# A one-core transformer layer on Trainium2: a rewritten drain, single signals, and two transposes in front of the first feed-forward product

## The reference

```python
# x: ids (128, 128); D = 64, four heads of 16, hidden 256
h = tok(x)        # 3 table rows per id -> 3 products + gelu -> fused product + gelu
                  # -> layer norm -> * (id != 0);  h = item_emb + 0.1 * fused
h = h + attn(layernorm(h))     # per sequence: softmax(q k^T / 4) v, then Wo
x3 = layernorm(h)
weights = x3 @ wr + br                        # one number per token
_, idx = top_k(weights, 64); sel = idx[:63]   # the 63 largest of a sequence's 128
y = gelu(x3[sel] @ w1 + b1) @ w2 + b2
out = h + x3;  out[sel] += y * weights[sel]
```

## Time and profile before

| | us |
|---|---|
| median of 3 runs | 552.93 |
| lowest, highest | 550.33, 558.99 |
| the profiled execution's own time | 557.61 |
| its span, first to last instruction | 555.7 |
| PE busy | 456.0 (82%) |
| DVE busy | 420.0 (76%) |
| ACT busy | 377.8 (68%) |
| POOL busy | 350.6 (63%) |

### The profile page before, as it was taken

The page is one execution under the profiler, slowest core; times in us unless marked ns, Lnnn a source line. Parts: engine busy times, 40 slices in busy tenths (PEclk is TensorE's granted clock), DMA queues, the critical chain, the costliest instruction groups (busy, mean ns, idle before and its releaser), DMA issues. The chain is left out here.

```text
span 555.7 us, 16674 instructions
## 1 busy us (share of the span) xinstructions
PE 456.0 (82%) x5850; PEld 346.8 (62%) x5850; DVE 420.0 (76%) x1648; ACT 377.8 (68%) x662; POOL 350.6 (63%) x412
## 2 busy tenths in 40 slices
PE   4778788888898888988988988888988789968670
PEld 2445576676666566766666666666767666756460
DVE  1367788877877888888777777888886658887486
ACT  1236677787877777777877778777776667846550
POOL 5746676676666676666766676667666547541574
PEclk9788999999999999999999999999997889998855
DMA  3211111111111111111111111111111111000046
GB/s 96 31 21 28 27 21 19 26 23 23 23 23 23 23 17 18 18 17 23 23 23 23 23 23 23 23 17 18 18 17 21 23 20 14 13 2 3 21 122 162
DMA packets 23733, 15.72 MB, mean 28 GB/s; under 512 B 18848, under 2 KB 21536, under 8 KB 23712
## 3 DMA queue, kind: packets, MB, share of 16 engines
q0 software_dynamic: 6144, 9.97, 12.1%
q1 hardware_dynamic: 17568, 5.48, 3.7%
HBM read 10.98 MB, written 4.19 MB: 27 GB/s over the span
## 5 line engine op out<-in xcount | busy, mean ns | idle before, releaser
L335 POOL TENSOR_TENSOR rs<-ve,minus_half 128x4 f32<-128x4 f32 x96 | 103.8, 1091 | 68.6 <-DVE ve L677 67.2
L327 POOL DMA_INDIRECT G<-table,idx x64 | 66.2, 1034 | 57.6 <-issue 47.7
L770 DVE TENSOR_REDUCE neg_max<-psum 128x4 f32<-128x512 f32 x128 | 84.4, 680 | 5.4 <-PE psum L1124 5.4
L327 POOL DMA_INDIRECT G<-turned,idx x64 | 60.7, 948 | 19.5 <-issue 19.5
L1052 PE MATMUL psum<-wt,hid 128*128 128x64 f32 x512 | 69.8, 294 | 2.5 <-ACT hid L471 1.5
L464 ACT ACTIVATE prob<-psum 128x512 f32<-128x512 f32 x128 | 66.1, 602 | 5.3 <-PE psum L1094 3.5
L1052 PEld LDWEIGHTS psum<-wt,hid 128*128 128x128 f32 x512 | 66.1, 208 | 3.3 <-ACT hid L471 2.2
L1094 PE MATMUL psum<-q_s,k_s 32*128 32x128 f32 x1024 | 39.1, 288 | 28.6 <-issue 23.5
L1094 PEld LDWEIGHTS psum<-q_s,k_s 32*128 32x128 f32 x1024 | 33.4, 191 | 35.5 <-issue 29.2
L814 DVE TENSOR_SCALAR k_s<-psum,wt 128x512 f32<-128x512 f32 x32 | 24.0, 751 | 31.7 <-PE psum L1211 31.0
L1124 PE MATMUL psum<-k_s,q_s 32*128 32x128 f32 x1024 | 41.1, 301 | 3.5 <-ACT prob L464 3.5
(11 more groups left out here) (116 smaller groups left out, 1108.5 us busy)
## 6 DMA issues: line engine op xcount, KB each, us to landing
out<-R SPq DMA_DIRECT2D x13, 256.0 KB, 2.6
G<-table,idx POOLq DMA_INDIRECT x64
G<-turned,idx POOLq DMA_INDIRECT x64
wt<-packed SPq DMA_DIRECT2D x1, 932.0 KB, 4.8
q_s<-max_t SPq DMA_DIRECT2D x32, 8.0 KB
out<-R SPq DMA_DIRECT2D x1, 512.0 KB, 4.3
out<-R SPq DMA_DIRECT2D x2, 128.0 KB, 3.5
ids_sb<-ids SPq DMA_DIRECT2D x1, 64.0 KB, 1.9
```

The costliest lines, as they stand in the source:

```text
L327: pool.indirect_dma_start(G[par][:, b, :], None, turned if b >= 2 else table, bass.IndirectOffsetOnAxis(ap=idx[par][:, b:b + 1], axis=0),) ...
L335: pool.tensor_tensor(rs[:, :], ve[:, :], minus_half[:, :], ALU.pow).then_inc(S[dst], 1)
L770: dve.tensor_reduce(neg_max[:, GB * h:GB * h + GB], bank[h].rearrange("p (b k) -> p b k", b=GB), AX, ALU.max, negate=True).then_inc(S["max ...
```

## The change

1. *Order on PE.* In a step `attention_t` and `fused_t` stand in front of `ffn_first`, which stood ahead of them.
2. *Single signals.* `scores`, `scores_back`, `queries`, `keys` and `ffn_first` signal once, at their last matmul, where they signalled four, four, two, two and four times; the waits count accordingly.
3. *Where the loops end.* PE's and DVE's loops end at step 17 (SPLIT = 18) and steps 18 to 29 are written out on both. ACT, POOL and SP keep theirs.
4. *Routing in three parts.* Part 0 is now columns 0 to 63 and is ranked by DVE inside the written-out steps: weights taken in step 18, one round in each of steps 19 to 25, selection in 26, coefficients in 27. Part 1 is columns 64 to 119, ranked in the drain. The last two groups (columns 120 to 127) are not ranked by rounds: PE spreads each weight column over a 128 x 128 block (`wide`) and DVE counts for every token how many of its sequence's weights lie above it (`compare`), ties broken by position with a triangular mask `lower` made in the setup.
5. *The end.* POOL scales and adds ten items of eight columns from step 29 on, the last after its last `add_x3`; ACT scales five; DVE adds six, and for the last group adds b2 times the coefficient to R ahead (`shift_routed`) and then the product straight from PSUM (`finish`). Stores follow a new order.
6. *The drain's order.* W's transposition moves behind `maxima_t` of the last group, ACT's table loads and copies change places, and five small matmuls (`keep_busy`) stand between the last products.

```diff
+HALF = P // 2
+TAIL = P - 2 * GB
+PARTS = ((0, HALF), (HALF, TAIL))
+SPLIT = 18
...
             def scores_t(odd, at):
...
-                    if at == GB - 1:
-                        last.then_inc(S["st_ready"], 1)
+                if at == GB - 1:
+                    last.then_inc(S["st_ready"], 1)
```

PE's step and the call of its pipeline:

```diff
             def step(i, odd, half):
...
-                if on(d):
-                    ffn_first(d)
                 if on(e):
                     attention_t(e)
                 if on(a):
                     fused_t(a)
...
+                if on(d):
+                    ffn_first(d)
                 if on(c):
                     scores_back(c, odd)
+                if type(i) is int and i == SPLIT:
+                    wait(pe, "qs_ready", 1, b)
+                    weights_t(0)
+                    pe.wait_ge(rank_in, 1)
+                if type(i) is int and i == SPLIT + KEEP // 8 + 2:
+                    wait(pe, "qs_ready", 1, b)
+                    coefficients(0)
+                    pe.wait_ge(coef_ready, 1)
                 if on(b):
                     v_product(b)
...
-            pipeline(pe, step)
+            pipeline(pe, step, end=SPLIT)
```

DVE's step, and the comparison that is new on it:

```diff
             def step(i, odd, half):
...
                 if on(e):
                     divide(e)
+                if type(i) is int and SPLIT < i <= SPLIT + KEEP // 8:
+                    rounds(0, i - SPLIT - 1, i - SPLIT)
+                if type(i) is int and i == SPLIT + KEEP // 8 + 1:
+                    select(0)
                 if on(b):
                     keys_out(b, odd)
...
+                if type(i) is int and i == SPLIT:
+                    take_weights(0)
+                if type(i) is int and i == SPLIT + KEEP // 8 + 2:
+                    take_coef(0)
                 if on(b):
                     v_out(b, odd)
...
+            def compare(g):
+
+                dve.wait_ge(wide_ready, g - TAIL // GB + 1)
+                for b in range(GB):
+                    wide, own = bank[RANK_BANK[g]][:, b * P:(b + 1) * P], wb[g % 2][:, b:b + 1]
+                    last = dve.scalar_tensor_tensor(equal[:, b, :], wide, own, lower[:, :],
+                                                    ALU.is_equal, ALU.mult)
+                done(last)
...
+                done(dve.tensor_reduce(rank[:, :], above[:, :, :], AX, ALU.add))
+                dve.scalar_tensor_tensor(of(coef, g), rank[:, :], float(KEEP), wb[g % 2][:, :],
+                                         ALU.is_lt, ALU.mult).then_inc(rank_done, 1)
```

274 lines of the change are left out of this document (163 added, 111 removed).

## The result

The changed kernel takes 575.5 us (median of 4, 573.4 to 576.8) beside 555.7 for the kernel before (median of 4). The ratio is 1.038 with the interval [1.032, 1.044]: slower by about 20 us, where 20 us less had been forecast. (The fourth run of the kernel before moves its median from 552.93 to 555.7.) Each later set of runs, which the expectations name a call, was measured side by side on one chip. One set met the kernel before at 528.8 us instead of 555 to 559, so every kernel is read against the kernel before of its own set.

A forecast was written before the change was run, and what follows sets the result against it. The prediction saw a chain through all four engines, each near eight tenths busy, not one engine. Gains 8.7 + 7.7 - 2.8 + 5.0 + 1.9 = 20.5 us gave span 535.2 and a median of about 532, range 518 to 547.

The forecast's parts named there:

- The step that failed: Looped steps: the moved product ends later, hidden by ACT's table load; without that cover it would cost 0.6 us.
- rival C: Written-out steps: PE's code comes late or its clock halves, 5.4 us per stop; slower, median 597 at worst; chance 0.06.
- Rival A: Loop: the maxima's DMA or POOL's gathers take the freed place, loop gives 1 us; median 543; chance 0.22.
- The evidence against it: Profiled steps 28 and 29, DVE and POOL outside their loops: same DMA and gathers at a 14.21 us period.
- POOL allows 0.9: Looped steps: DVE can come about 0.9 us earlier before POOL becomes what rm waits for.
- the 0.62 forecast: Looped steps 4 to 17: gain per step from transposes ahead of the product; 14 steps give 8.7 us.
- The ranking in the steps: Steps 18 to 27: rounds free in DVE's idle time; selection, PE's two stops and setup cost 2.8 us.
- Written-out code and the single signals: Steps 18 to 29 written out: gain 7.7 us; single signals: priced at 0, with 0 to 0.3 a step for the range.
- The forecast -5.0: Drain up to the last o_t: waits for W and x3 and four rounds go; gain 5.0 us, bounds 2 and 6.5.
- the 1.9 forecast: From the last o_t to the end: 22.0 us against 23.9, gain 1.9, bounds -1 and 4.
- the stores behind as before (4.2): End of the kernel: the stores after DVE's last add still take 4.2 us.
- I take it as chance: DVE's 2.95 us stop before 438.33 and clock 0.50 from 440 to 445 us, taken as explaining the 4.7 us distance to the median.

The follow-up runs named there:

- fewer waits: Three redundant waits removed from GpSimd's fetch: kernel before 525.3 us, changed kernel 518.4 us in one set; changed kernel 573.1 us in a later set.
- one gather: One gather of a group's rows instead of four, the rest of the tile constant: kernel before 516.1 us, changed kernel 502.0 us.
- the transposes in between: Kernel before with the attention transposes between the two halves of the first feed-forward product: 551.8 us, ratio 0.987.

## Why the prediction was wrong

The table gives each term of the sum, in us of the profiled spans: as forecast, and as measured with the hold (changed against before), without it (both with fewer waits), and with one gather, where there is none either.

| | forecast | hold | no hold | one gather |
|---|---|---|---|---|
| up to k_s no. 5 | 0 | +4.0 | -1.1 | -0.5 |
| 14 looped steps | -8.7 | +9.9 | -1.1 | -7.5 |
| 12 further steps | -4.9 | +7.7 | +0.8 | -3.0 |
| last k_s to last o_t | -5.0 | -3.1 | -1.8 | -6.1 |
| last o_t to the end | -1.9 | -0.3 | -0.3 | -0.1 |
| sum | -20.5 | +18.1 | -3.5 | -17.1 |

**The step that failed** is one sentence in the looped steps: the product ends later, "its reader on ACT stands behind a table load of its own, which hides it. Without that cover it would cost what it is later, 0.6." The table load does hide it where the signal comes through: gelu at 1.68 in all looped steps without the hold. With the hold the signal comes 2 us late, the gelu at 3.1 or 3.8, and 0.6 was no bound: a step has that wait, a stop of PE and, in about every third step, 5 us at clock 0.50. In the looped steps that last item is the loss (+10.8 us in the five steps with a lowered clock, -0.9 in the other nine); the forecast had a stop with half a clock only as a chance event and in rival C, which it tied to late code. In the order before, the product's signals had left PE by 0.8 us after k_s and got through; the new order put them into the hold.

**Rival A named the place and not the price.** It said that the gathers might hold o_t to the end of a gather's issue, and concluded that then nothing is won. What held o_t could hold any of PE's signals: o_t left the hold, the product entered it. The evidence against it, came from one step in which this signal got through, and in which the third gather stood at 0.38 after k_s instead of 0.62. The trace had a warning in it: in the earlier trace rows L1028 ends at 327.37 and DVE, idle, starts the copy 0.49 later, just as GpSimd's third issue ends (326.88 + 0.94 in the same trace). No dependence in the program explains that half microsecond, and the prediction booked it to PE's order.

**What was next behind o_t** was also missed. The prediction wrote that POOL allows 0.9 and took a period of 14.45. Without the hold the old order already runs at 14.15 (o_t at 1.16, not 1.61), so most of the distance from 15.07 to 14.2, which the prediction gave to PE's order, was the hold's. The new order runs at 14.07: POOL starts its power 0.17 us after the fourth gather ends, and rm waits 0.47 for it. In the old order POOL itself waits 0.47 for DVE's variance at this place, and the step is the same with one gather, 14.16. Only in the new order do the gathers stand in the way; with one gather it takes 13.62, and the order shows its worth, 0.54 a step. That this lies near the 0.62 forecast is in part luck, since the 0.62 was worked out from a step that the hold had lengthened. In the kernel with four gathers and no hold it is 0.08 a step.

**The ranking in the steps** was priced at 2.8. With one gather, step no. 19, where PE waits for the transposed weights, is 1.1 longer than its neighbours (14.71 against 13.6), no. 28 with the coefficients 0.3, the two before it 0.15 each: 1.7, so that was somewhat dear. Step no. 29 is 1.1 longer than in the kernel before (14.87 against 13.80); POOL's first scale and add stand in it, which the prediction had not priced. **Written-out code and the single signals** were rightly priced at nothing.

**The drain.** The forecast -5.0 came out as -1.8 to -6.1, inside its bounds of 2 and 6.5 but for a little. The spread follows the clock of this stretch: the kernel before took 26.3 us at a mean clock of 0.88 and 28.5 at 0.75 (one gather), the changed one 22.5 at 1.00 (one gather), 23.2 at 0.93 and 24.5 at 0.90. At the two most alike, 0.88 and 0.90, the gain is 1.8, so the 5.0 was probably too high. DVE's tail gained 3.1, more than the 1.9 forecast: the passes over PSUM took 0.28 each as assumed, and only two instructions were drawn out beside GpSimd (1.23 and 1.37 us instead of 0.42). But "the stores behind as before (4.2)" was wrong. What sets the end is when the last uninterrupted run of stores can start, and that moved by 0.4 only (18.4 instead of 18.8 after the last o_t), with the two comparisons ahead of most of DVE's last sums; that these are the reason is argued, not tested.

**Rival C** had the shape of the loss (a stop, then half the clock, again and again) and the wrong cause, code that comes late, and so a chance of 0.06. **"I take it as chance"**, of the stop near 438, was wrong in part: a pause of GpSimd recurs in the step before it in every run with that many gathers (see the last section), though not every kernel has the long stop behind it.

What stays open: by what path the gathers hold PE's signals and PE's queue, why one set of six was free of it, and when a stop of PE is followed by the half clock. Another place for the gathers, which would avoid it, needs a third buffer for their rows, and that was not tried.

## What to carry to other kernels

An instruction that is moved takes its completion signal to a new moment: look at what every other engine is doing then, in this kernel GpSimd's gathers, and not only at who waits for it. An idle piece of half a microsecond in front of an instruction whose input is already there is a finding that has to be explained before anything is moved into its neighbourhood. And behind the wait that goes, price the next one by its row: here POOL left 0.08 us of 0.54 a step, and the stores 0.3 of 3.1.

## What the hardware showed that was not expected

**Signals of PE held during gathers.** In five of six sets of runs PE's signals sent later than about 1 us after k_s were seen at about 1.7, 2.4, 3.1 or 3.8, whatever they carried, while GpSimd issued gathers (0.95 us each, at -2.0, -0.6, 0.65 and 1.9). DVE's waits on itself in the same stretch stayed at about 0.15 us. In one set the same program ran without any of it. For the kernel before this is 528.8 against 555 to 559 us, so the state is worth 5% of a kernel that was not changed at all, and it decides what this change is worth: 0.987 [0.974, 1.001] without it, level or a little faster, and 1.034 [1.024, 1.043] with it, for the same edit.

**A pause at the 114th gather.** In every recorded run that issued that many gathers, with the hold and without, GpSimd stands 2.1 us before its 114th, the second of its group, where every other second gather of a group has 0.30. First the kernel before, then the changed one with fewer waits in the set without the hold:

```profile
414.85 1.07 POOL L327 DMA_INDIRECT G<-table,idx  x1 [1.26 <-issue]
418.05 0.96 POOL L327 DMA_INDIRECT G<-table,idx  x1 [2.13 <-issue]
419.31 0.95 POOL L327 DMA_INDIRECT G<-turned,idx  x1 [0.30 <-issue]
```

```profile
387.71 1.11 POOL L332 DMA_INDIRECT G<-table,idx  x1 [0.97 <-DVE idx L838]
390.90 0.95 POOL L332 DMA_INDIRECT G<-table,idx  x1 [2.09 <-issue]
```

The step of the second block is 15.5 us long instead of 13.8, and nothing else happens. In the kernel before, the pause shifts the last two gathers into another part of the step, the next step follows with the 2.95 us of the earlier trace rows and the half clock of the earlier trace rows, and the two steps are 7.9 us longer than two others. That stop does not always follow: with the transposes in between, under the hold as well, the same two steps took 15.87 and 15.23. The pause comes between 391 and 548 us, by the kernel, so it isn't tied to time; and in the runs with 32 or 64 gathers the same place of the program has none. That it goes by the number of gathers is argued from this; what is counted is not known.
